# Decay's running sums by a VectorE scan instead of TensorE products with a triangular matrix

## The reference, cut to what matters

```python
w = -jax.nn.softplus(-(w0 + jnp.tanh(xw @ w1) @ w2)) - 0.5
wd = jnp.exp(-jnp.exp(rs(w)))
def step(S, xs):
    r_, w_, k_, v_, a_, b_ = xs
    sa = jnp.einsum('bhij,bhj->bhi', S, a_)
    S = S * w_[:, :, None, :] + sa[..., None] * b_[:, :, None, :] + v_[..., None] * k_[:, :, None, :]
    y = jnp.einsum('bhij,bhj->bhi', S, r_)
```

## Time and profile before

| | |
|---|---|
| runs | 546.82, 549.33, 551.17 us |
| the profiled execution | 544.08 us, span 542.0 us |
| granted TensorE clock, mean | 0.883 |
| PE busy | 445.7 us (82%) |
| DVE busy | 286.5 us (53%) |
| ACT busy | 200.2 us (37%) |
| POOL busy | 159.4 us (29%) |

### The profile page before, as it was taken

How to read it: one execution, slowest core, us unless ns; L and a number is a source line. 1 busy time by engine, 2 the same in 40 slices (tenths; PEclk the granted TensorE clock), 3 DMA queues, 4 the chain that set the end, 5 groups by cost and what they waited for, 6 DMA issues and landing times.

```text
span 542.0 us, 23307 instructions
## 1 busy us (share of the span) xinstructions
PE 445.7 (82%) x10731; PEld 352.9 (65%) x10731; DVE 286.5 (53%) x656; ACT 200.2 (37%) x397; POOL 159.4 (29%) x141
## 2 busy tenths in 40 slices
PE   0588999999999999999999987937547999999800
PEld 0457686687787887777786766724324799999700
DVE  2557795865875957857747652135353233222212
ACT  0384744645636637447336320024200222222100
POOL 5736143431523442244313311010055000000073
PEclk9987999999999999999799985767855699999955
DMA  9700000000000000000000000008052276676245
GB/s 302 258 10 3 4 5 4 5 4 6 4 5 4 5 5 4 4 5 5 2 4 5 5 4 5 2 2 310 1 184 98 84 220 212 202 225 200 79 132 178
DMA packets 20810, 37.85 MB, mean 70 GB/s; under 512 B 2800, under 2 KB 14570, under 8 KB 20714
## 3 DMA queue, kind: packets, MB, share of 16 engines
q1 hardware_dynamic: 18378, 30.07, 17.4%
q0 software_dynamic: 2336, 6.30, 3.7%
HBM read 26.14 MB, written 10.22 MB: 67 GB/s over the span
## 4 chain that ended last, share of the span: by engine, by line
PE 74%; DVE 11%; issue 4%; POOL 4%; ACT 3%; DMA 3%; POOLq 0%; DVEq 0%; ACTq 0%
PE ps L1185 8%; PE ps L1196 7%; PE ps L801 6%; PE ps L794 6%; PE ps L904 3%; PE ps L1164 3%; POOL arena L333 3%; PE ps L806 2%; PE ps L1042 2%; PE ps L813 2%; PE ps L880 1%; DVE arena L516 1%; PE ps L1138 1%; PE ps L972 1%; PE ps L845 1%
## 5 line engine op out<-in xcount | busy, mean ns | idle before, releaser
L516 DVE SCALAR_TENSOR_TENSOR arena<-arena 128x256 f32<-128x256 f32 x96 | 47.5, 543 | 6.0 <-PE ps L845 5.0
L1185 PEld LDWEIGHTS ps<-arena 128*128 128x128 f32 x368 | 46.5, 199 | 1.6 <-issue 0.5
L1185 PE MATMUL ps<-arena 128*128 128x128 f32 x368 | 46.8, 282 | 0.1
L333 POOL DMA_INDIRECT arena<-sorted_o,arena x16 | 15.8, 985 | 102.5 <-DMA sorted_o<-arena 98.0
L1196 PE MATMUL ps<-arena 128*128 x184 | 43.5, 380 | 0.1
L475 ACT COPY arena<-ps 128x256 f32<-128x256 f32 x23 | 8.6, 373 | 86.1 <-PE ps L1174 86.1
L794 PE MATMUL ps<-arena 128*128 128x256 f32 x128 | 36.5, 435 | 2.5 <-issue 2.5
L801 PE MATMUL ps<-arena 128*128 128x256 f32 x128 | 36.8, 436 | 1.3 <-ACT arena L452 0.8
L1196 PEld LDWEIGHTS ps<-arena 128*128 128x128 f32 x184 | 33.2, 190 | 4.2 <-issue 0.6
L761 DVE TENSOR_TENSOR arena<-ps,arena 128x512 f32<-128x512 f32 x23 | 15.9, 692 | 35.1 <-PE ps L1185 35.1
L794 PEld LDWEIGHTS ps<-arena 128*128 128x128 f32 x128 | 26.2, 215 | 7.9 <-issue 3.1
(11 more groups left out here) (260 smaller groups left out, 1063.7 us busy)
## 6 DMA issues: line engine op xcount, KB each, us to landing
arena<-W SPq DMA_DIRECT2D x23, 514.0 KB
arena<-W SPq DMA_DIRECT2D x8, 512.0 KB, 6.6
sorted_x<-arena SPq DMA_DIRECT2D x1, 2944.0 KB
arena<-sorted_x SPq DMA_DIRECT2D x23, 128.0 KB, 3.9
sorted_o<-arena SPq DMA_DIRECT2D x23, 128.0 KB, 3.6
out<-arena SPq DMA_DIRECT2D x16, 128.0 KB
arena<-W SPq DMA_DIRECT2D x4, 256.0 KB, 4.5
arena<-consts SPq DMA_DIRECT2D x1, 738.5 KB, 4.2
```

Source lines behind the costliest of these rows:

```text
L333: pool.indirect_dma_start(out=back[:, t, :], out_offset=None, in_=sorted_o[:, :], in_offset=bass.IndirectOffsetOnAxis(ap=place[:, t:t + 1] ...
L516: last = V.scalar_tensor_tensor(out=mix[j % 3][:, p, :], in0=xx[:, p].rearrange("p b t -> p (b t)"), scalar=mixed_by[MIXES[j]][:, p:p + 1] ...
L1185: last = mm(ps[:, 2 + b, m * 128:(m + 1) * 128], W1_s[q % WB][:, p * HID + m * 128:p * HID + (m + 1) * 128], x_sT[b][:, p, :], start=p == ...
```

## The change

P.cum leaves PE. DVE takes it over with one scan instruction, `state = keep * state + sigmoid`, over 128x512 elements; `keep` is a new constant, 0 at the first step of each run of 64 and 1 elsewhere, which restarts the sum. The scan needs the sigmoids by channel with time along the free side, so P.wup's product is made by channel (the weights w2 are now the stationary side), w0 becomes the bias of ACT's sigmoid, and ACT writes in two pieces in the scan's order. P.decay reads the sums from SBUF: `prod` in one piece, `invp` in two. The row of ones that carried w0 is gone (w2 has 64 rows, not 65). In `ORDER`, P.cum moves one place forward, to stand before Q.X3.

```diff
-P.key:1 P.wup:1 Q.W0:0 O.zT:-1 P.lg:1 Q.X3:0 P.cum:1 P.vc:1 P.decay:1 Q.T3:0 P.rt:1 Q.A0:0 P.kP:1 P.ar:1 P.tokk:1
+P.key:1 P.wup:1 Q.W0:0 O.zT:-1 P.lg:1 P.cum:1 Q.X3:0 P.vc:1 P.decay:1 Q.T3:0 P.rt:1 Q.A0:0 P.kP:1 P.ar:1 P.tokk:1
-HEADED = ["k_k", "k_a", "a0"]
-CONSTS = [("ident", 128), ("ones_bd", 128), ("tri", B * SL), ("within", 2 * L), ("pairs", L), ("eye", L), ("low", 4 * L), ("iota", E),
+HEADED = ["k_k", "k_a", "a0", "w0"]
+CONSTS = [("ident", 128), ("ones_bd", 128), ("keep", GR * SL), ("within", 2 * L), ("pairs", L), ("eye", L), ("low", 4 * L), ("iota", E),
...
-        v, v2nd, vgate, sig_w, gate, rtv = (carve(CH, C) for _ in range(6))
+        v, v2nd, vgate, gate, rtv = (carve(CH, C) for _ in range(5))
+        sig_w, cum = carve(2, B, SL), carve(2, B, SL)
...
                 elif step == "P.wup":
                     act.wait_ge(s["wup_ps"], n)
-                    A.activation(flat(sig_w), ps[:, 3, :], ACT.Sigmoid).then_inc(s["sig_ok"], 1)
+                    for h2 in range(2):
+                        last = A.activation(sig_w[:, h2].rearrange("p b (c t) -> p c b t", c=CH), pair(ps[:, 3, :], h2).rearrange("p (c b t) -> p c b t", c=CH, b=B),
+                                            ACT.Sigmoid, bias=head_of["w0"][:, h2:h2 + 1])
+                    last.then_inc(s["sig_ok"], 1)
...
                 elif step == "P.decay":
-                    act.wait_ge(s["cum_ps"], n)
+                    act.wait_ge(s["cum_ok"], n)
+                    A.activation(prod[par][:, :, :, 1:SL + 1], cum, ACT.Exp, scale=DECAY)
                     for h2 in range(2):
-                        last = A.activation(prod[par][:, h2, :, 1:SL + 1].rearrange("p b (c t) -> p c b t", c=CH),
-                                            pair(ps[:, 2, :], h2).rearrange("p (c b t) -> p c b t", c=CH, b=B), ACT.Exp, scale=DECAY)
-                    last
-                    A.activation(invp, ps[:, 2, :], ACT.Exp, scale=-DECAY).then_inc(s["invp_ok"], 1)
+                        last = A.activation(pair(invp, h2).rearrange("p (c b t) -> p c b t", c=CH, b=B), cum[:, h2].rearrange("p b (c t) -> p c b t", c=CH),
+                                            ACT.Exp, scale=-DECAY)
+                    last.then_inc(s["invp_ok"], 1)
...
+                elif step == "P.cum":
+                    dve.wait_ge(s["sig_ok"], n)
+                    after(dve, "invp_ok", i)
+                    V.tensor_tensor_scan(cum.rearrange("p h b x -> p (h b x)"), cst["keep"], sig_w.rearrange("p h b x -> p (h b x)"), 0.0,
+                                         ALU.mult, ALU.add).then_inc(s["cum_ok"], 1)
...
                 elif step == "P.wup":
-                    up_by_token(w2_sb, low_w, 3, 65).then_inc(s["wup_ps"], 1)
+                    for h2 in range(2):
+                        last = mul(pair(ps[:, 3, :], h2), w2_sb[0:64, h2 * 128:(h2 + 1) * 128], low_w[0:64, :], start=True, stop=True)
+                    last.then_inc(s["wup_ps"], 1)
...
-                elif step == "P.cum":
-                    pe.wait_ge(s["sig_ok"], n)
-
-                    for h2 in range(2):
-                        mul(pair(ps[:, 2, :], h2), sig_w[:, 0, h2 * 128:(h2 + 1) * 128], cst["tri"], start=True, stop=False)
-                        last = mul(pair(ps[:, 2, :], h2)[:, 128:256], sig_w[:, 1, h2 * 128:(h2 + 1) * 128], cst["tri"][:, 0:128], start=False, stop=True)
-                    last.then_inc(s["cum_ps"], 1)
...
-        "tri": ((row[:, None] // L == pos[None, :] % 128 // L) & (t[:, None] <= pos[None, :] % L + L * (pos[None, :] // 128))).astype(f),
+        "keep": np.broadcast_to((np.arange(GR * SL) % SL > 0).astype(f), (128, GR * SL)),
```

More of the change, by code:

```diff
@@ L176, in build @@
         mom1_ok sd1_ok rstd1_ok lessm_ok xn_ok xT_ps xT_carry xT_ok xx_ok mix_ok k_ps kk_ok sq_ok r_ps v_ps v_ok lv_ps lv_ok
-        vd_ok lwa_ps la_ok vga_ps a_ok t1_ok vg_ok vs_ok v2_ok wup_ps sig_ok lg_ps g_ps g_ok cum_ps invp_ok nrm_ps nmax_ok
+        vd_ok lwa_ps la_ok vga_ps a_ok t1_ok vg_ok vs_ok v2_ok wup_ps sig_ok lg_ps g_ps g_ok cum_ok invp_ok nrm_ps nmax_ok
         lnk_ok key_ok rk_ok ar_ok rt_ps rt_ok kP_ok bP_ok tokk_ps tokk_ok tokb_ps tokb_ok vsum_ok vmean_ok vc_ok rtv_ok
@@ L223, in _ @@
                 sp.dma_start(dst, src[:, :, :]).then_inc(s["weights_in"], 16)
-            for dst, src, rows in ((w2_sb, w2, 65), (a2_sb, a2, 128), (v2_sb, v2, 33), (g2_sb, g2, 128)):
+            for dst, src, rows in ((w2_sb, w2, 64), (a2_sb, a2, 128), (v2_sb, v2, 33), (g2_sb, g2, 128)):
                 sp.dma_start(dst[0:rows, :], src[:, :]).then_inc(s["weights_in"], 16)
@@ L501, in _ @@
             V.memset(low_v[32:33, :], 1.0)
-            V.memset(low_w[64:65, :], 1.0)
             for par in range(2):
@@ L786, in _ @@
             mul = functools.partial(nc.tensor.matmul, skip_group_check=True)
-            tri_1 = cst["tri"].rearrange("p (b x) -> p b x", b=B)[:, :, 0:L]
             r_k_of = cst["r_k_of"]
@@ L1253 @@
         "W": np.stack([two(a[P + "W" + c]) for c in "rkvo"]),
-        "w1": two(a[P + "w1"]), "w2": np.concatenate([a[P + "w2"], a[P + "w0"].reshape(1, C)], axis=0),
+        "w1": two(a[P + "w1"]), "w2": a[P + "w2"],
         "a1": two(a[P + "a1"]), "a2": np.concatenate([a[P + "a2"]] * 2, axis=0),
```

## The result

The change makes the kernel slower. Four runs gave 576.82, 578.14, 581.29 and 582.97 us, median 579.71; the kernel before gave 543.98 to 551.17 us, median 548.08. The ratio on record is 1.070 (95% interval 1.064 to 1.076); the two medians alone make 1.058. The profiled execution took 578.14 us with a span of 576.4 us, against 544.08 and 542.0 us, which makes 1.063. Medians here are of all runs of a kernel and ratios of its fast runs alone, so a ratio need not be the quotient of two medians. From which runs of the kernel before the 1.070 comes is not on record.

A forecast was written before the change was run, and what follows sets the result against it. PE bounds nearly everywhere, but before Q.T3 DVE and PE end together. 544.08 + 0.4 (constants) + 5.6 (scan) + 23.8 (clock) = 573.9 us; 576 us was taken, between 573.9 and 579.1, range 553 to 586.

The forecast's parts named there:

- the scan is free: First turn, before any Q step: DVE waits for POOL between L565 and L625 anyway, so the scan adds nothing.
- 0.4 us for the constants: At the start: the wider `keep` loads 131 KB more ahead of the first weights; 0.4 us, bounds 0 and 0.5.
- a fall: PE's clock dropping to half between Q.T3 and P.k; priced at 4.2 us, up to 4.7, in each of seven turns.
- The products were not on the chain: Before Q.T3: P.cum's PE products fill a wait for DVE; removing them gains at most 0.8 us in three turns.
- The scan costs 1.15 us of DVE's chain: Before Q.T3: the scan delays DVE's copy by 1.15 us, fully in four turns, partly in three; +5.6 us.
- The clock is the largest term: Between Q.T3 and P.k: waits among small PE products lower the clock in seven turns; 29.4 us, +23.8 us of it new.
- ACT holds for P.kP by 0.2 us: Behind Q.T3: P.decay's result reaches P.kP in time by about 0.2 us; cost taken as 0.
- The sigmoid in two pieces and the product by channel: On ACT and PE: sigmoid some 0.3 us longer but with slack, P.wup's products as many and as wide; both 0.
- a value between two bases: Final step: 576 us, between 573.9 us on the profiled execution's time and 579.1 us if other runs' extra time stays.
- The pause of 1.16 us: PE's pause at 82 us, right behind full-size products, passed without a clock fall; evidence that the clock might hold.
- rival 1: The scan lengthens DVE's chain before Q.T3 but the clock holds; 555 us, chance 0.15.

The follow-up runs named there:

- e7: Changed kernel with the scan done twice, the first into a buffer nobody reads; median 589.17 us, ratio 1.084 to the kernel before.
- e1: Changed kernel plus four full-size PE products nobody reads, between Q.X3 and Q.T3; median 558.69 us, ratio 1.027 to the kernel before.
- e2: Changed kernel without the scan, P.decay taking exp of the plain sigmoids (another output); median 563.68 us, ratio 1.041 to the kernel before.
- e6: Changed kernel with DVE's operations reordered to shorten its chain before Q.T3, plus four unread full-size PE products there; median 542.93 us, ratio 0.999 to the kernel before.
- e4: Changed kernel with DVE's operations reordered to shorten its chain before Q.T3, no products added; median 552.45 us, ratio 1.023 to the kernel before.
- e5: Kernel before the change with only DVE's operations reordered, P.cum staying on PE; median 541.47 against 542.61 us, ratio 0.997.
- e3: Changed kernel with P.cum back at its old place behind Q.X3, so DVE scans after the masked copy; median 566.63 us, ratio 1.045 to the kernel before.
- e8: Changed kernel with DVE's operations reordered and P.g's two needed products moved between Q.X3 and Q.T3; median 542.53 us, ratio 0.998 to the kernel before.

## Where the prediction was right, and the step that failed

The mechanism was right and its sum too small. The step that failed is *"In the first turn, before any Q step runs, DVE waits for POOL at this place and the scan is free"*: the first slab was put at nothing but 0.4 us for the constants, and it came 2.5 us later than priced (point 5). The largest term was mis-sized as well: a fall was priced at 4.2 us, at most 4.7, and costs 5.1 us (point 3). And the forecast said less than its own sum (point 6).

1. *The products were not on the chain; PE's saving is no gain.* Right: PE waits instead.
2. *The scan costs 1.15 us of DVE's chain, 5.6 us in seven turns.* Right in size. The scan takes 1.21 us, and the turn without a fall is 38.28 us against 37.54 us before (predicted 38.3). e7 shows the limit of it: in turns that fall anyway, a further scan costs 0.3 us a turn, not 1.15.
3. *The clock is the largest term, +23.8 us.* Right in kind: e1, e2 and e6 show that taking the falls away takes the cost away. A fall was priced at 4.2 us and costs 5.1 us, with the clock low for 10.2 or 13.65 us, not 6.7. It came in six turns, not seven. So the two errors cancel for the most part, which is luck: 6 x 5.1 = 30.6 us against 7 x 4.2 = 29.4 us. From the first Q.T3 to the eighth the time grew by 293.11 - 263.87 = 29.2 us. These seven stretches hold six of the seven scans that delay a Q.T3 (the seventh stands ahead of the first one), so the prediction has 29.4 - 1.15 = 28.3 us for them.
4. *ACT holds for P.kP by 0.2 us.* Right: in the turn without a fall ACT ends at 251.96 and P.kP starts at 252.19 us. The sigmoid in two pieces and the product by channel cost nothing that e6 could tell.
5. *The first slab.* This step failed. The first Q.T3 starts at 76.71 instead of 72.64 us, 4.07 us later, where 0.4 us for the constants and 1.15 us for the scan right ahead of it were priced. The timelines of DVE and POOL, before, after, and in e2 (no scan):

```profile
13.63 0.69 DVE L527 TENSOR_TENSOR arena<-arena 128x512 f32<-128x512 f32 x1 [7.97 <-DMA arena<-table,arena]
...
38.69 3.34 POOL L298 TENSOR_TENSOR arena<-arena 128x512 f32<-128x512 f32 x1 [3.55 <-ACT arena L394]
...
43.42 0.69 DVE L581 TENSOR_REDUCE arena<-arena 128x8 f32<-128x512 f32 x1 [2.51 <-POOL arena L300]
```
```profile
15.22 0.69 DVE L530 TENSOR_TENSOR arena<-arena 128x512 f32<-128x512 f32 x1 [9.05 <-DMA arena<-table,arena]
...
39.98 4.41 POOL L299 TENSOR_TENSOR arena<-arena 128x512 f32<-128x512 f32 x1 [3.55 <-ACT arena L395]
...
45.76 0.69 DVE L589 TENSOR_REDUCE arena<-arena 128x8 f32<-128x512 f32 x1 [2.44 <-POOL arena L301]
```
```profile
39.49 3.34 POOL L299 TENSOR_TENSOR arena<-arena 128x512 f32<-128x512 f32 x1 [3.55 <-ACT arena L395]
```

The gathered rows came 1.6 us later in this execution, of which 1.3 us are left when DVE reaches the slab's P steps. In e1 to e4, which have the same constants, they came 0.3 to 0.7 us later, and in e5, which has the old ones, 0.7 us, so this is mostly the execution's own and no run shows the 0.4 us. POOL's operation took 4.41 instead of 3.34 us while DVE worked on beside it, scan included; it takes 3.34 us again in e2, without the scan, and 4.41 us in e3, with it. So the scan was not free: DVE waited for POOL, and POOL was held up by the scan, for 1.07 us. Another 0.6 us pass up to the next turn's P.key with the clock at 0.50 from 42.6 to 52.8 us; before, it was low in 3.7 us of that time. The clock's term was missing for the first slab altogether. Why the clock is low so long there stays open: e1, which has products there again, was low from 35.4 to 52.4 us. The last 1.14 us are the scan right ahead of this Q.T3.

6. *The base.* The sum itself has 29.8 us of change over an execution of 544.08 us, 5.5%. The forecast, 576 us, stood beside a median of 549.33 us: 26.7 us, 4.9%. By taking a value between two bases it gave away 3.1 us of its own sum. By executions the change cost 34.1 us. The 4.3 us over the sum are 2.5 us of the first slab, 1.0 us of the seven stretches, and 0.8 us behind the last Q.T3 and outside the span. By medians it cost 31.6 us. The ratio on record would be some 38 us; the rest of that stays open. The runs of the kernel before spread from 536.6 to 556.7 us over all comparisons, and their granted clock goes with it in the main (536.63 us at 0.902, 550.05 us at 0.863).

The pause of 1.16 us that no fall followed was the argument for rival 1. e1 shows how much it is worth: waits of up to 1.6 us, with full-size products right ahead of them, do not come free either, only cheaper.

## What to carry to other kernels

Before work is taken off the busiest engine, look at whether the chain of waits passes through it at that place. If another engine ends at the same moment there, the work was filling a wait, and giving its replacement to that other engine lengthens the path. And where TensorE does small products with pauses between them, the few full-size ones among them may be what keeps its clock up: look at the granted clock around them before removing or moving them. Needed products that can be moved there do it (e8, 0.998), but they leave a thin place where they came from; useless ones did as well here (e6, 0.999).

## What the runs showed of the hardware

- TensorE can be at half its clock while it is busy without a pause: 10.00 us of 10.00 in e2, 13.65 of 13.65 in the changed kernel, both at small products and then at full-size ones that take twice their time.
- The low clock costs more than the work whose removal brought it on: 1.5 us of products removed, 5.1 us paid in a turn with a fall.
- What a fall costs goes with how long the low clock lasts: 2.3 us for 6.8 us in e1, 4.0 us for 10.2 us in e4, 5.1 us for 10.2 to 13.65 us in the changed kernel.
- VectorE can hold up GpSimd: GpSimd's operation of 128x512 in the first slab took 3.34 us without the scan beside it (before, e2) and 4.41 us with it (the changed kernel, e3).
- A scan of 128x512 on VectorE takes 1.21 us, 1.8 times a plain 128x512 operation (0.68 us), and its time does not spread: 1210 to 1218 ns over eight.
